# The gathers of a tensor product: in one run of 54 a chunk, or in blocks of six that wait for folds

## What is computed

```python
# cut; h = relu(layernorm(x)), per edge e: src[e], dst[e], a distance and a vector
R = relu(abs_distances[:, None] @ w1 + b1) @ w2 + b2     # (edges, 384)
Fj = features[src]                                       # a gather, 32 floats an edge
for each pair (lo, li) of the irreps and each filter lf:
    acc += NORM * einsum('euv,ef,evi,ofi->euo', Rb[..., k], Yf, Fb, C)
out = zeros.at[dst].add(msg)                             # (nodes, 32)
```

## Time and profile before

| | us |
|---|---|
| median of three runs | 12342.97 (12339.77 to 12357.08) |
| the profiled execution's own time | 12262.02 |
| its span, first to last instruction | 12256.3 |
| tensor product, first gather to last gather's start | 5097.0 to 11930.8 |
| mean granted TensorE clock | 0.646 |

### The profile page before, as it was taken

The page is one execution under the profiler, slowest core; times in us unless marked ns, Lnnn a source line. Parts: engine busy times, 40 slices in busy tenths (PEclk is TensorE's granted clock), DMA queues, the critical chain, the costliest instruction groups (busy, mean ns, idle before and its releaser), DMA issues. The chain is left out here.

```text
span 12256.3 us, 73033 instructions
## 1 busy us (share of the span) xinstructions
PE 3840.2 (31%) x20408; PEld 3120.5 (25%) x20408; DVE 5220.4 (43%) x6900; ACT 1898.2 (15%) x1882; POOL 6351.7 (52%) x6677
## 2 busy tenths in 40 slices
PE   1000000000000000145555555464555555464544
PEld 0000000000000000034444444343444444343433
DVE  2233333333333334244544545454545445454544
ACT  0122222222222222000100101010100001010101
POOL 6766666666666666544444343434444443434343
PEclk5555555555555555577777777777777777777777
DMA  5333333434333434111111111111111111111111
GB/s 214 80 97 98 99 97 98 99 95 99 98 98 98 100 99 105 29 33 36 42 38 39 40 37 40 37 44 34 43 35 42 41 37 40 37 44 33 44 36 38
DMA packets 400152, 794.13 MB, mean 65 GB/s; under 512 B 164767, under 2 KB 242319, under 8 KB 388095
## 3 DMA queue, kind: packets, MB, share of 16 engines
q1 hardware_dynamic: 157528, 459.39, 14.0%
q0 software_dynamic: 213216, 166.16, 8.3%
q10 hardware_dynamic: 29382, 168.33, 3.4%
HBM read 499.75 MB, written 293.61 MB: 65 GB/s over the span
## 5 line engine op out<-in xcount | busy, mean ns | idle before, releaser
L969 POOL DMA_INDIRECT feat<-scratch_h,src x3132 | 2965.9, 947 | 3910.6 <-DMA src<-in_src 2973.0
L522 POOL DMA_INDIRECT kv<-scratch_kv,src_i x3132 | 2983.5, 953 | 1564.1 <-issue 973.4
L1210 DVE TENSOR_TENSOR prod<-psR,ops 128x384 f32<-128x384 f32 (+1 forms) x3132 | 1922.6, 681 | 3138.6 <-remote 2395.0
L995 PE MATMUL psS<-prod,ident 128*128 128x192 f32 x11136 | 2092.2, 348 | 2057.0 <-issue 1872.9
L995 PEld LDWEIGHTS psS<-prod,ident 128*128 128x128 f32 x11136 | 2018.8, 207 | 2144.0 <-issue 2116.8
L781 PE MATMUL psA<-ident,tail 128*36 128x128 f32 x3 | 0.8, 414 | 4553.0 <-DVEq L806 4553.0
L984 PE MATMUL psR<-whigh,stack 128*128 128x384 f16 x3132 | 1083.6, 347 | 452.8 <-issue 261.0
L1088 ACT ACTIVATE red<-psS,scales 128x192 f32<-128x192 f32 x522 | 219.9, 421 | 6071.6 <-remote 3522.0
L781 PEld LDWEIGHTS psA<-ident,tail 128*36 128x36 f32 x3 | 0.3, 129 | 4553.1 <-DVEq L806 4553.1
L985 PE MATMUL psR<-wlow,capped 128*128 128x384 f16 x3132 | 1082.7, 346 | 173.5 <-issue 172.9
L624 DVE TENSOR_TENSOR sq<-attr 128x162 f32<-128x162 f32 x58 | 19.0, 328 | 1870.9 <-DMA attr<-in_attr 1634.8
(11 more groups left out here) (253 smaller groups left out, 3875.2 us busy)
## 6 DMA issues: line engine op xcount, KB each, us to landing
w_row<-in_wT SPq DMA_DIRECT2D x232, 432.0 KB
stack<-scratch_hid SPq DMA_DIRECT2D x174, 576.0 KB
scratch_state<-out ACTq DMA_DIRECT2D x58, 1080.0 KB
scratch_qexp<-zeros ACTq DMA_DIRECT2D x32, 1566.0 KB
kv<-scratch_kv,src_i POOLq DMA_INDIRECT x3132
qin<-scratch_qexp SPq DMA_DIRECT2D x58, 864.0 KB
scratch_hid<-high SPq DMA_DIRECT2D x232, 216.0 KB
scratch_hid<-low SPq DMA_DIRECT2D x232, 216.0 KB
```

The costliest lines, as they stand in the source:

```text
L522: nc.gpsimd.indirect_dma_start(kv[b][:, t, :], None, a["kv"], bass.IndirectOffsetOnAxis(ap=src_i[b][:, t:t + 1].bitcast(U32), axis=0)).the ...
L969: nc.gpsimd.indirect_dma_start(feat[b][:, t, :], None, a["h2"], bass.IndirectOffsetOnAxis(ap=src_i[b][:, t:t + 1].bitcast(U32), axis=0)).t ...
L995: nc.tensor.matmul(psS[:, 0:GC].rearrange("p (t c) -> p t c", c=COLS), ident[:, :], prod[r][:, :, j, :], start=(n == 0), stop=False)
L1210: v.tensor_tensor(to[:, :, :, lo:lo + n], psR[:, g % 2, :, frm:frm + n * JC].rearrange("p t (j u) -> p t j u", j=JC), ops[b][:, ts, x * JC ...
```

## The change

POOL's 54 gathers of a chunk are cut into nine blocks of six (SIX = 6). Ahead of each block POOL waits for `prod_ready`, at a count that the fold of a certain step reaches: for block k of chunk c this is the fold of step k+4 of chunk c-2, where steps from 9 on are those of chunk c-1 (PACE = 4). It also increments `chunk_begun` ahead of each block. `prod_ready` is now primed with 18, two chunks' worth, so that the first chunks' blocks pass, and PE's wait for `prod_ready` is raised by the same 18.

```diff
+PACE = 4
...
                         pool.wait_ge(feat_free, i * 2 + b + 1)
                         pool.sem_inc(chunk_begun, 1)
                         for t in range(T):
+                            if t % SIX == 0:
+                                pool.wait_ge(prod_ready, (i * 2 + b) * SPC + t // SIX + PACE + 1)
+                                pool.sem_inc(chunk_begun, 1)
                             nc.gpsimd.indirect_dma_start(
                                 feat[b][:, t, :], None, a["h2"],
...
-                    pe.wait_ge(prod_ready, q + 1)
+                    pe.wait_ge(prod_ready, q + 2 * SPC + 1)
...
                 for primed, n in ((feat_free, 2), (prod_done, 6), (sum_free, 2), (ops_free, 2),
-                                  (red_free, 2), (scanned, 1), (run_copied, 1)):
+                                  (red_free, 2), (scanned, 1), (run_copied, 1), (prod_ready, 2 * SPC)):
```

## The result

The changed kernel takes 11574.61 us (median of four, 11542.08 to 11591.62); the kernel before, run beside it, 12341.37 us (12337.38 to 12357.08). The ratio is 0.937, with a 95% interval of 0.936 to 0.938: 767 us gained, where 1848 were forecast, and 25 us above the upper end of the range. The profiled execution took 11542.08 us (span 11536.1), 720 us less than the profiled one of before.

A forecast was written before the change was run, and what follows sets the result against it. Engines' instructions were taken to come late during POOL's gather runs. At 9.6 us a step, 86.4 a chunk, 33.0 us saved in 56 chunks gives 1848: 12343 - 1848 = 10495 us, range 9600 to 11550.

The forecast's parts named there:

- What bounds the kernel: Tensor product: engines' instructions come late while POOL gathers; a chunk takes 119.36 us, nearly nothing happening for 63 us.
- the gathers are the bound: Rival, chance 0.15: engines never starve in blocks, POOL runs through; 67.5 to 70.7 us a chunk, 9439 to 9618 us.
- Free terms: Priming and PE's raised wait cancel, costing nothing; POOL's nine waits and increments add 0 to 3.2 us a chunk.
- Block 8: Waits for step 3's fold, needed by DVE at step 5: 11.4 us available, 9.4 needed, so hidden.
- The lag: Supply returns 9.8 us after a 67.25 us run, 0.146 of it; for a block an estimated 1.05 us.
- Stores: Ready instructions keep engines going 9.3 us into a run after the shortest refill; within 8.3 us they hold.
- 8.9 us if each block has died away before the next, and folds gate it so: One step with a block in it: 7.2 gathering + 1.05 late supply + 0.66 waits; starving stops folds, so POOL pauses.
- The clock: PE's lower clock makes a step 8.2 to 12.4 us, middle 10.3; averaged with 8.9 to 9.6 us.
- Half a step falls outside: Forecast's far end: ACT's or DVE's store empties in mid-block; 11.7 us a step, 105 a chunk, 11548 us.
- Every block stops the engines at once: Slower rival, chance 0.13: nine short starvings a chunk, 15.1 us a step, 136 a chunk, 13286 us.
- The stalls hang on something else, such as the loops: Rival, chance 0.04: the change only moves gathers, and time stays at 12343 us, within 0.2%.
- A or B: Experiments' theories: A, gathers pile up a backlog that shuts off instructions; B, a gather in progress shuts off the supply.

The follow-up runs named there:

- the kernel before on the third chip: The kernel before, run unchanged on a third chip for a trace of its own: 8637.29 us.

## Why the prediction was wrong

**What bounds the kernel: right, for the executions it read.** The engines' instructions come late while a run of gathers is on; cut the runs and the time falls. The new trace shows it again, with the clean start (12 us, in the earlier trace rows 13.6) and the return after the run. One of the readings was weak: 0.33 and 0.70 us in the earlier trace rows belong to two different transfers, and the second (L474) takes 0.51 to 1.33 us also where nothing starves (the kernel before on the third chip, 2517.33 to 2659.47). The same trace holds the better rows. SP issues the same small loads of the attention two times, 67 to 82 us into a run of gathers and then in the silence after it:

```profile
3005.76 0.70 SPq L489 DMA_DIRECT2D dst_i<-in_dst_ext  x1
3009.96 0.70 SPq L490 DMA_DIRECT2D dst_i<-in_dst  x1
3014.86 1.40 SPq L492 DMA_DIRECT2D attr<-in_attr  x1
3020.46 0.70 SPq L495 DMA_DIRECT2D qin<-scratch_qexp  x1
...
3091.99 0.33 SPq L489 DMA_DIRECT2D dst_i<-in_dst_ext  x1
3092.50 0.33 SPq L490 DMA_DIRECT2D dst_i<-in_dst  x1
```

They come 4.2 to 5.6 us apart during the run and 0.51 us apart in the silence. That it is the supply of instructions, and not something else that slows every engine's stream, remains a reading: no experiment acted on it. Not foreseen was that this is no property of the kernel alone: elsewhere the same gathers leave DVE fed. The forecast says nothing of such a chip, where it would have been "the gathers are the bound" for both kernels.

**Free terms: right.** The priming, PE's raised wait and the nine waits cost nothing seen on the chips where nothing starves (68.5 us a chunk with or without gates, inside 67.5 to 70.7). Block 8 is hidden: L1185 waited 50.6 us for gathers in the whole program, once. The margin was 2.0 us by the forecast (11.4 against 9.4); one fold less of lead made it 3.7 us late.

**The lag: right.** 0.146 of a run was taken; 3.4 us after 22.4 us is 0.15.

**Stores: right in kind, short in size.** They were to hold 9.3 us; they held about 12. In all 163 runs DVE's silence begins right behind a fold and PE's just ahead of L999, so it is the place in the program that counts as well as the time.

**The step that failed: "8.9 us if each block has died away before the next, and folds gate it so".** The gate counts folds, not time. The argument "when the engines starve, no fold comes, POOL pauses" is true, but only from the first starving on, 12 us into a run. A clean step takes 6.88 us by the earlier trace rows, the folds of such a run come 4.4 to 8.8 us apart (5.7 and 7.1 in the one shown), and a block takes 7.5 us; so by the time of the starving two more folds have been given, and a run is three blocks. Both numbers, 6.88 and 9, stood in the prediction, and a table of which fold permits which block would have shown it. Put together for merged blocks: a run of 18 takes 22.4 us, and the prediction's own lag gives 0.146 x 22.4 = 3.3. From DVE's return to the next run are 10.0 us, which no term of the prediction gives; it is read from the trace. That makes 35.7 us for three steps, 11.9 a step, against the 9.6 forecast. A gain of 12.8 us a chunk is left (120.2 - 107.4) and not 33.

**The clock: right in sign.** 9.6 us contained 0.7 us for it. PE's granted clock rose only from 0.75 to 0.81 over the stage, and a restart finds it low, now three times a chunk: those 20 matmuls take 2.9 us more (6.28 against 3.41). How much of that DVE waits for wasn't separated. The factor of 1.33 was misread as that of the half clock: the 24 matmuls of 5.45 us in the earlier trace rows are a mix of both levels. Ahead of them PE's matmuls start 0.32 us apart (9175.79, 9176.11), behind them 0.16 (9183.00, 9183.16), a factor of 2.

**The rivals.** "Half a step falls outside" gives 11.7 us a step and 11548 us: its price was met (11575) by luck, for its mechanism was not: the blocks didn't stand alone. "The gathers are the bound" did come true, on the other chips. "Every block stops the engines at once" fell: the start of each run is clean. "The stalls hang on something else, such as the loops" fell too: the loops run alike on chips where the kernel takes 8637 us, and moving the gathers moved the stalls. The rule of the Trainium skill (Runtime: NRT & Kernel Launch, Instruction fetch mechanics) by which refills hide behind the issue rate agrees with the runs on those chips (DVE's products wait 12.5 us in all) and not with the executions first profiled, where PE idled 13.10 us for "issue". The count of packets on the instruction queue, on which the prediction leaned, decides nothing: it is 20 in the changed kernel's first trace, and 20 in its trace where nothing starves.

**Open.** What makes an execution starve: whether another user of the chip, its memory or a setting, no view shows. The chip of the first executions isn't on record, so it is open too whether the chip or the time made the difference. Whether blocks kept apart by a pause of POOL's own would end the starving, by A or B, wasn't tried where it occurs.

## What to carry to other kernels

If blocks are released by another engine's progress, write down which event permits which block: where a block takes longer (7.5 us) than the event's period (5.7 and 7.1 us in the run shown), blocks merge until something else stops them. Idle time whose releaser is "remote" or "issue" on several engines at once may be no dependence of the kernel, as it was none here; run the unchanged kernel on a second chip before pricing a change against it. And a pause that helps under such a disturbance is a price everywhere else: 17 us a chunk here for a 2.2 us pause behind every sixth gather.

## What the runs showed of the hardware that was not expected

- The same program takes 12341 us in one place and 8634 to 8651 us on seven chips, each with a spread within 0.2%. In the slow place every engine's instructions come late during POOL's gathers: SP's issues 4.2 to 5.6 us apart where they are 0.51 apart in the silence.
- Semaphore waits and increments on POOL between gathers are hidden where nothing starves (68.5 us a chunk with none, one a block, or five a gather), while a wait for a memset of its own costs 0.61 us a gather.
- A plain copy of 128 rows issued by POOL takes 0.537 us, the gather of as many rows 0.96 us.
